# Gate and up products of tile pairs in seven products of 256 columns

## The reference

```
x = x + layernorm(attention(layernorm(x), w_qkv, w_dense))
h = silu(g) * u;  g = xq @ w1.T;  u = xq @ w3.T;  y = hq @ w2.T
x = x + layernorm(y)
```

## Time and profile before

| | |
|---|---|
| median of three runs | 1111.55 us (1110.86 to 1112.1) |
| the profiled execution, its own time | 1111.28 us |
| its span, first to last instruction | 1109.5 us |
| mean granted clock of TensorE | 0.998 of full speed |
| busy: PE, PE weight loads, DVE, ACT, POOL | 1088.5, 908.3, 858.3, 674.9, 768.8 us |

### The profile page before, as it was taken

The page is one execution under the profiler, slowest core; times in us unless marked ns, Lnnn a source line. Parts: engine busy times, 40 slices in busy tenths (PEclk is TensorE's granted clock), DMA queues, the critical chain, the costliest instruction groups (busy, mean ns, idle before and its releaser), DMA issues.

```text
span 1109.5 us, 16613 instructions
## 1 busy us (share of the span) xinstructions
PE 1088.5 (98%) x5134; PEld 908.3 (82%) x5134; DVE 858.3 (77%) x1740; ACT 674.9 (61%) x1320; POOL 768.8 (69%) x765
## 2 busy tenths in 40 slices
PE   9999999999999999999999999999999999999997
PEld 7888888888888888888888888888887778888885
DVE  5635566667899899989999999997687966666666
ACT  6533233327989798888788898885677532222215
POOL 6844447537768878869799799787845755666635
PEclk9999999999999999999999999999999999999999
DMA  6444474455889899898998989984210133333422
GB/s 231 129 176 152 150 235 138 143 152 199 293 296 344 291 317 336 287 346 281 319 353 305 319 313 319 339 277 154 97 58 1 38 115 119 119 109 84 121 64 98
DMA packets 163537, 227.86 MB, mean 205 GB/s; under 512 B 37761, under 2 KB 126465, under 8 KB 158593
## 3 DMA queue, kind: packets, MB, share of 16 engines
q1 hardware_dynamic: 163456, 226.88, 60.9%
HBM read 130.50 MB, written 96.34 MB: 204 GB/s over the span
## 4 chain that ended last, share of the span: by engine, by line
PE 86%; DVE 5%; POOL 2%; ACT 2%; DMA 2%; issue 1%; POOLq 0%; DVEq 0%; SPq 0%
PE psS L1636 24%; PE psT L1636 16%; PE psOY L1636 16%; PE psOY L1773 15%; PE psOY L1788 14%; PE psT L1754 2%; DMA p_scr_long<-probs_long 1%; DVE y L1429 1%; DMA squares_long<-p_scr_long 1%; DVE oT_lo L1284 1%; ACT probs_long L1065 1%; PE psS L1648 0%; POOL x L893 0%; POOL qT_lo L687 0%; DVE squares_long L1371 0%
## 5 line engine op out<-in xcount | busy, mean ns | idle before, releaser
L1065 ACT ACTIVATE probs_long<-probs_long,negmax 128x896 f32<-128x896 f32 (+9 forms) x124 | 122.2, 987 | 6.4 <-DVE negmax L1352 6.0
L687 POOL TENSOR_TENSOR pT_lo<-squares_long,pT_hi 128x896 fp32r<-128x896 f32 (+3 forms) x47 | 108.2, 2309 | 25.2 <-ACT pT_hi L1060 25.0
L748 POOL TENSOR_SCALAR probs_short<-probs_short,rsum 128x256 f32<-128x256 f32 (+9 forms) x128 | 75.9, 605 | 47.9 <-DVE rsum L1359 47.7
L815 POOL TENSOR_SCALAR hidden<-mask,hr,hs 128x128 f32<-128x128 f32 x112 | 49.2, 449 | 85.2 <-DVE hr L1449 85.2
L1788 PE MATMUL psOY<-wd_hi,oT_hi 128*128 128x512 f32 x256 | 103.5, 404 | 2.2 <-DVE oT_lo L1284 1.8
L1371 DVE STREAM_TRANSPOSE squares_long<-squares_long 128x1792 f32<-128x1792 f32 (+3 forms) x54 | 101.6, 1882 | 0.9 <-DMA squares_long<-p_scr_long 0.9
L1114 ACT ACTIVATE mask<-psS 128x256 f32<-128x256 f32 x56 | 21.5, 383 | 130.8 <-PE psS L1636 130.8
L1788 PE MATMUL psOY<-wd_hi,oT_lo 128*128 128x512 f32 x256 | 100.2, 391 | 0.0
L1788 PE MATMUL psOY<-wd_lo,oT_hi 128*128 128x512 f32 x256 | 100.1, 391 | 0.0
L1636 PE MATMUL psS<-kT_hi,qT_hi 128*128 128x512 f32 (+5 forms) x280 | 98.2, 351 | 1.3 <-DVE negmax L1352 0.7
L748 POOL TENSOR_SCALAR probs_long<-probs_long,rsum 128x896 f32<-128x896 f32 (+9 forms) x70 | 74.6, 1068 | 33.2 <-DVE rsum L1359 32.9
(11 more groups left out here) (216 smaller groups left out, 3389.4 us busy)
## 6 DMA issues: line engine op xcount, KB each, us to landing
q_raw<-q_scr SPq DMA_DIRECT2D x64, 256.0 KB, 5.1
p_scr_long<-probs_long SPq DMA_DIRECT2D x14, 896.0 KB, 5.7
squares_long<-p_scr_long SPq DMA_DIRECT2D x14, 896.0 KB, 6.9
p_scr_long<-probs_long SPq DMA_DIRECT2D x12, 1024.0 KB, 6.0
squares_long<-p_scr_long SPq DMA_DIRECT2D x12, 1024.0 KB, 6.8
p_scr_long<-probs_long SPq DMA_DIRECT2D x14, 768.0 KB, 5.5
squares_long<-p_scr_long SPq DMA_DIRECT2D x14, 768.0 KB, 4.4
raw<-in_w_qk SPq DMA_DIRECT2D x10, 1024.0 KB, 6.3
```

The costliest lines, as they stand in the source:

```text
L687: return nc.gpsimd.tensor_tensor(dst, source, hi.bitcast(F32), ALU.subtract)
L748: nc.gpsimd.tensor_scalar(row, row, rsum[:, column(t, u)], 1.0, ALU.mult, ALU.mult).then_inc(p_ready[lane(t)], 1)
L815: last = nc.gpsimd.tensor_scalar(to, columns_of(h_sb[:, m % 2, b * P:(b + 1) * P], to), hr[:, m % 2, b:b + 1], hs[:, m % 2, b:b + 1], ALU. ...
L1065: nc.scalar.activation(row, row, ACT.Exp, bias=negmax[:, column(t, u)], scale=-1.0, accum_out=lsum[:, column(t, u)]).then_inc(e_done[lane( ...
```

## The change

From chunk 2 on (FIRST_W = 2) tiles are taken in pairs. The tokens of the two tiles, the two halves of the 512 inputs, and gate and up form a 2 x 2 by 2 x 2 block product, made with seven products and sums: each has 2 blocks of inputs x 3 passes = 6 matmuls of 256 columns. Per pair 42 matmuls of 256 columns stand where 24 of 512 stood. `down` stays as it is.

```diff
+        W_BANKS = {"P1": psT[:, 0, :], "P2": psT[:, 0, :], "P6": psT[:, 1, :], "P7": psS[:, 0, 0:BANK], "P5": psS[:, 0, BANK:S],
+                   "P4": psS[:, 1, 0:BANK], "P3": psS[:, 0, BANK:S]}
+        W_ORDER = ("P1", "P6", "P7", "P5", "P4", "P2", "P3")
...
+            for n in range(FIRST_W * NT, C * NT, 2):
...
+                for name in W_ORDER[:5]:
+                    half_product(n, name)
+                half_product(n, "P2")
+                next_down(n - LAG)
+                half_product(n, "P3")
+                if n == C * NT - 2:
+                    pe.wait_ge(w_summed, sum_count(n, "up_early"))
+                    turn_last(n - 1, (n - 1) % 2)
+                next_down(n + 1 - LAG)
```

DVE makes five sums for each pair and the hidden values of both tiles at once; the two `turn_hidden`, `lo_of_hidden` and `add_down` stay:

```diff
+            def make_pair(n):
+                dve.wait_ge(g_done, n + 2)
+                dve.wait_ge(h_ready, n)
+                dve.wait_ge(w_summed, sum_count(n, "up_late"))
+                nc.vector.tensor_tensor(h_sb, ups[:], g_sb, ALU.mult).then_inc(h_made, 2)
...
+                block_max(h_sb.rearrange("p s c -> p (s c)"), top).then_inc(h_step, 2)
...
+                block_scale(scale, top).then_inc(h_step, 2)
...
+                nc.vector.reciprocal(inverse, scale).then_inc(h_scaled, 2)
...
+            for n in range(FIRST_W * NT, C * NT, 2):
+                if n > FIRST_W * NT:
+                    add_or_finish(n - 1 - LAG)
+                    turn_hidden(n - LAG, n - LAG, loads_of(n - LAG))
+                sum_of_products(n, "both")
+                if n > FIRST_W * NT:
+                    lo_of_hidden(n - LAG, n - LAG)
+                sum_of_products(n, "three")
+                turn_hidden(n - LAG + 1, n - LAG + 1, loads_of(n - LAG + 1))
+                sum_of_products(n, "up_early")
+                lo_of_hidden(n - LAG + 1, n - LAG + 1)
+                sum_of_products(n, "gate_early")
+                if n < C * NT - 2:
+                    add_or_finish(n - LAG)
+                    if n == C * NT - 4:
+                        make_hidden(n, 0)
+                    sum_of_products(n, "up_late")
+                    if n == C * NT - 4:
+                        make_hidden(n + 1, 1)
+                    else:
+                        make_pair(n)
```

Each sum is one instruction of 256 columns with one operand in PSUM and one in SBUF. The weights' sums T1 to T4 are made by POOL (four subtractions of 512 elements a partition and chunk) and split like blocks B11, B21 and B22: seven casts on ACT and seven low parts on POOL where four stood. The scaling moves from POOL (one instruction a piece) to ACT (four of 128 columns a piece):

```diff
+            POOL_WORK = {1: ("T1", "T3", "T2", "T4"), 3: ("B11", "B21", "B22", "T3"), 5: ("T1", "T2", "T4", "D0"), 7: ("D1",)}
...
+            ACT_WORK = {0: (0, 1), 1: (2, 3), 2: ("B11", "B21"), 3: ("B22", "T3"), 4: ("T1", "T2"), 5: ("T4", KT), 6: (KT + 1, "D0"),
+                        7: ("D1",)}
...
+                for j in range(BANK // P):
+                    block_ = source[:, j * P:(j + 1) * P]
+                    last = nc.scalar.activation(block_, block_, ACT.Copy, scale=table[:, col + j:col + j + 1])
...
+            for n in range(FIRST_W * NT, C * NT, 2):
+                c, i = n // NT, n % NT
+                copy_first(n)
+                if n > FIRST_W * NT:
+                    hi_of_hidden(n - LAG, n - LAG)
+                prepare(c + 1, i)
+                hi_of_hidden(n - LAG + 1, n - LAG + 1)
+                silu_early(n)
...
+                silu_late(n + 1)
+                prepare(c + 1, i + 1)
```

The hidden tile's way through DRAM is regrouped on the way out, so that one DMA brings it back where four did; from chunk 2 on both tiles of a pair leave before they are fetched:

```diff
-                for c in range(HG):
-                    sp.dma_start(hidden[c * SPAN:(c + 1) * SPAN, slot, :].rearrange("q (a x) -> q a x", a=HG),
-                                 h_scr[slot, :, c * CW // HG:(c + 1) * CW // HG].rearrange("(a q) x -> q a x", a=HG)
-                                 ).then_inc(h_in[slot], 16)
+                sp.dma_start(hidden[:, slot, :], h_scr[slot].rearrange("c (q a) x -> (c q) (a x)", a=HG)
+                             ).then_inc(h_in[slot], 16)
```

More of the change, by code:

```diff
@@ L67, in sandwich_kernel @@
     LAST_TURNS = 3
-    CENTERED = NT - 3
+    CENTERED = NT - 4
     SPAN = P // HG
@@ L280, in sandwich_kernel @@
         x1 = at("x1", 198, [P, NT, D])
+        x32 = [at(f"x32_{p}", 146 + 4 * p, [P, 2, KT, P]) for p in range(NT // 2)]
+        sT = [at(f"sT_{p}", 32 + 16 * n, [P, 4, 2, BANK], F32R) for n, p in enumerate(PARTS)]
+        later = [[at(f"later{e}_{p}", (68, 146)[e] + 6 * n, [P, 3, 2, CW], F32R) for n, p in enumerate(PARTS)]
+                 for e in range(2)]
+        t_sums = {t: at(f"sum_{t}", kb, [P, 2, CW]) for t, kb in (("T1", 178), ("T2", 180), ("T4", 30))}
+        first, both, three = (at(n, 80 + k, [P, CW]) for k, n in enumerate(("first", "both", "three")))
+        gate_early, ups = at("gate_early", 83, [P, CW]), at("ups", 158, [P, 2, CW])
         spare = [214 * KB]
@@ L981, in _ @@
                     norms(*item)
[L983 to L987 removed]
+            for c in range(1, C - 1):
+                feed_forward_chunk(c)
+            feed_forward_last()
             finish(CENTERED - 1)
@@ new lines, in hi_of_half, with copy_first, silu_early @@
+            def hi_of_half(p):
+                act.wait_ge(half_made, 5 * p + 4)
+                sums = x32[p][:].rearrange("p e (n k) c -> p (e n) k c", k=2)
+                nc.scalar.copy(sT[0][:, :, :, p * P:(p + 1) * P], sums).then_inc(x32_made, 1)
+            def copy_first(n):
+                act.wait_ge(w_full, product_count(n, "P1"))
+                nc.scalar.copy(first[:], w_bank("P1")).then_inc(w_copied, 1)
+            def silu_early(n):
+                act.wait_ge(w_summed, sum_count(n, "gate_early"))
+                nc.scalar.activation(g_sb[:, n % 2, :], gate_early[:], ACT.Silu).then_inc(g_done, 1)
@@ L1573, in _, with loads_of, add_or_finish @@
             dve.wait_ge(d_done, NT - LAG)
[L1575 to L1587 removed]
+            def loads_of(n):
+                return 16 * (n // RING + 1)
+            def add_or_finish(n):
+                s = n - (C - 1) * NT
+                if s >= 0:
+                    finish(n, s)
+                else:
+                    add_down(n, n % NT)
             def finish(n, s):
@@ L1874, in _, with half_product @@
-            for n in range((C - 2) * NT, C * NT):
+            def half_product(n, name):
+                rows, weights = {"P1": ("A11", "B11"), "P2": ("A12", "B21"), "P3": ("S4", "B22"), "P4": ("A22", "T4"),
+                                 "P5": ("S1", "T1"), "P6": ("S2", "T2"), "P7": ("S3", "T3")}[name]
+                a, b = row_block(n % NT // 2, rows), weight_block(n // NT % 2, weights)
+                if name == "P2":
+                    pe.wait_ge(w_copied, pair_number(n) + 1)
+                if n > FIRST_W * NT:
+                    if name == "P1":
+                        pe.wait_ge(g_done, n)
+                    if name == "P6":
+                        pe.wait_ge(w_summed, sum_count(n - 2, "gate_early"))
+                    if name == "P5":
+                        pe.wait_ge(w_summed, sum_count(n - 2, "up_late"))
+                elif name == "P7":
+                    pe.wait_ge(h_made, n - 1)
+                elif name == "P4":
+                    pe.wait_ge(h_made, n)
+                if name == "P3":
+                    pe.wait_ge(w_summed, sum_count(n, "up_early"))
+                more = name in ("P2", "P3")
+                product(w_bank(name), [([t[:, k] for t in a], [t[:, k] for t in b]) for k in range(2)], start=not more,
+                        resumed=more).then_inc(w_full, 1)
@@ L1875, in _, with next_down @@
+            def next_down(n):
+                if n % NT == 0:
+                    pe.wait_ge(down_ready, (n // NT + 1) * CB)
+                down(n, n, n // NT % 2)
+            for n in range(NT, FIRST_W * NT):
                 if n % NT == 0:
                     pe.wait_ge(up_ready, (n // NT + 1) * KT)
-                if n % NT == LAG:
-                    pe.wait_ge(down_ready, (n // NT + 1) * CB)
-                step(n, n)
+                gate_up(n, n % 2, LAST[n % NT], up_w[n // NT % 2])
+                next_down(n - LAG)
```

375 lines of the change are left out of this document (248 added, 127 removed).

## The result

The changed kernel takes 1133.08 us in the median of four runs (1132.37 to 1135.17) beside 1111.82 for the kernel before (four runs, 1110.86 to 1112.56): ratio 1.0195, 95% interval 1.0177 to 1.0212. The forecast was 1107.1, range 1103 to 1116. So the sign was wrong, and the time lies 17 us above the range. The profiled execution has a span of 1130.6 us, 21.1 more than before's 1109.5.

The account below looks back on a forecast made before the run. PE was taken to bound the kernel, busy 98% of the span. Pairs -9.4, product changes +1, chunk 1 +0.8, transition +1.2 and end +2.0 sum to -4.4: 1111.55 becomes 1107.1 us, range 1103 to 1116.

Parts of the forecast that it names:

- The pairs: Steps 16 to 55: PE stays the bound, each pair falls from 8.16 to 7.69 us, 20 pairs save 9.4 us.
- slack: In each pair, DVE's up_early stands at 3.9 us and P3 wants it at 5.6: 1.6 us to spare.
- case 2: Pairs: DVE and POOL exclude each other in full, pair 8.0 us, whole 1113.5 or 1110.5 us; chance 0.22.
- Hidden behind PE; no cost: ACT in the pairs: up to 5.5 us of work in 7.69, including up to four weight pieces, costing nothing.
- product changes: Pairs: PE's changes from one of the seven products to the next lose 1 us over twenty pairs.
- Case 3: Pairs: POOL blocked too, its low part T4 late before a chunk's P1; pair 8.5, whole 1116 to 1122 us; chance 0.15.
- A narrow matmul: PE in the pairs: a matmul of 256 columns costs 0.118 us, against 0.227 for 512 columns.
- Chunk 1, +0.8: Steps 8 to 15: DVE needs 8.2 us a pair in 8.16, up_early comes late at step 16; loss 0.8 (0 to 2.5).
- Transition, +1.2: Out of attention: six more ACT casts of 512, two on the path at 0.6 each, cost 1.2 us (0 to 3.6).
- The end, +1.5: From step 54: last pair's tiles made singly, PE's transpose waits; 1.5 us against before, 2.0 with the counted saving.
- CENTERED: Behind the last matmul: takes 1.3 us off POOL, adds 0.7 to DVE; net 0 (-0.4 to +0.4).
- The ring: Hidden tile's store and fetch: back by 7 us of the next pair, wanted at 8.9, so free.

Follow-up runs that it names:

- e2: Changed kernel with POOL's sums and low parts of the weights of chunks 4 to 6 left out: 1127.3 us, beside 1113.42 for the kernel before.
- e6: Changed kernel with up tiles and turned hidden tiles in PSUM, ACT's high part ahead of weight pieces, chunk 2's raw weights loaded one tile earlier: ratio 1.0068 to before.
- e4: Changed kernel with ACT's high part of hidden tile n-3 ahead of the weight pieces and chunk 2's raw weights loaded one tile earlier: ratio 1.0159 to before.
- e10: Changed kernel with up tiles and turned hidden tiles in PSUM, ACT's order and raw weight load unchanged: 1122.2 us, beside 1113.65 for the kernel before.
- e1: Changed kernel with only the two up tiles moved from SBUF to a free PSUM bank: ratio 1.0128 to the kernel before.
- e13: Changed kernel with hidden tile 15 fetched back before tile 16 is stored, on SP: ratio 1.0173 to the kernel before.
- e15: Changed kernel with PSUM placement, later copies, reordered half sums, tile 15 fetched earlier and ACT's casts and weight pieces reordered: ratio 1.0003 to the kernel before.

## Why the prediction was wrong

- **The pairs, first failed step: "The means say 0.1 to 0.15 a blockable instruction today ... less than the slack. I take none of it for the end."** Measured: the product 0.50 above its 0.69, each low part 0.24 above its 0.41, the scale next to nothing: 1.0 us a pair in the mean in place of 0.5, and 2.0 in the slow pair shown above (1.56 for 0.69, 1.53 for 0.41). The pairs came 14.4 us above the forecast. I had written down that POOL would be at work right across these instructions, and still priced them by means from an order in which POOL was idle. The mechanism of case 2, which had 0.22, is what happened; the many short durations of before only said that the two seldom met. The Trainium skill (SBUF — State Buffer, "Who interferes with whom") states that the one that issues first keeps the other waiting for its whole instruction, and the trace agrees nearly: 1.53 us for 0.41 beside a subtraction of 1.3 begun 0.03 us earlier, where waiting for all of it would give 1.68. e2 (POOL's work gone) and e6 (DVE's second SBUF input gone) show it from both sides.
- **Case 2's own size, 8.0 a pair, was too low** (8.49): I had put the wait at P3 and given it all the 1.6 us of slack. The wait was at `down`, ahead of which the low part stands behind ACT's cast, which stands behind weights. "Hidden behind PE; no cost" for ACT's pieces failed here: 0.27 us a pair with the port (e4), 0.14 without (e10). Case 2's second time doesn't add up either: 1113.5 less product changes (1) and chunk 1 (0.8) is 1111.7, not 1110.5.
- **Case 3** gave the right pair, 8.5, for a wrong reason. POOL's low parts took 1.30 to 1.41 in most groups and PE never waited for T4.
- **A narrow matmul** was mis-sized a little: 0.119 to 0.120, not 0.118, and product changes cost nothing. The free pair is 7.80 where my terms gave 7.69 + 0.05; from before's 8.18 (mean of the 19 pairs) twenty pairs free of waits save 7.6 us, not 8.4.
- **Chunk 1, +0.8, was +8.2.** I added up 8.2 us of DVE in 8.16 as if nothing could block it, although each pair of steps has nine instructions of the kinds that POOL's can block (two scales, two low parts, four sums, the low part of 1024): POOL cost 5.5. The range (0 to 2.5) was made from the same unblocked sum. The wait of step 9, 2.4 to 2.5, I had not seen at all: I wrote of SP's loads that nothing queues behind them, and forgot ACT, whose list waits for the load with a cast behind it.
- **Transition, +1.2, was +4.2**, above my 0 to 3.6. I priced six casts by two that lay on the chain of before. Their own part is 2.4 to 2.9 us, within that range; the rest is the clock, see the last section, which had no term in my sum.
- **The end, +1.5 against before, was +2.1**, and 1.0 of it is again the blocked product (15.9 in e1, 15.8 in e6): without it my figure was 0.4 too high. Behind the last matmul 0.65 came on top, outside the 0 (-0.4 to +0.4) given for CENTERED; no run looked into it.
- **The first two pairs**: the fetch behind the store, 1.7 us (e13), was not seen. The ring I had called free is free in the steady state only: over all pairs DVE waited for a fetch once, these 1.9 us. About 1.3 us in the pair of step 16 is left in e15; DVE comes late out of chunk 1, and I did not settle it further.

## What to carry to other kernels

Price a shared port by where the other engine will be, not by how often the two met before: list the DVE instructions with two SBUF inputs, lay POOL's runs over them, and take the full block wherever they overlap. Moving one of the two inputs to a free PSUM bank takes the block away (8.49 to 7.95 us a pair in e10, which moves the up tiles and the turned tiles). And where an order changes its period, look at the first round for each queue: what now stands behind a wait that used to be short.
